# Second-layer attention on one core: the layer norm's last step on another engine, and the next chunk's projections at other steps

## What is computed

```
Q, K, V = relu(x @ Wq + bq), relu(x @ Wk + bk), relu(x @ Wv + bv)      # 16 heads of 8
scores = Q K^T / sqrt(8), masked (causal, and keys whose features sum to 0)
attn = softmax(scores) * query_mask
out = attn V + x
mean, var = mean(out), mean((out - mean) ** 2)                         # over the 128 features
normalized = (out - mean) / sqrt(var + 1e-8)
x = x + gamma * normalized + beta
layer = base_layer + einsum('bdr,bkr->bdk', x_a, x_b)                  # rank 8, one per sequence
x = x + x @ layer                                                      # then a slot-routing FFN
```

## Time and profile before

| | |
|---|---|
| median of 3 runs | 1248.66 us (1247.72 to 1248.96) |
| the profiled execution | 1247.93 us, of it the trace's span 1246.6 us |
| TensorE | 1078.6 us busy (87%) |
| VectorE | 983.2 us busy (79%) |
| ScalarE | 723.0 us busy (58%) |
| GpSimd | 567.7 us busy (46%) |
| the attention stage | first scores at 834.7, its last period begins at 1083.8, next stage at 1146.7 |

### The profile page before, as it was taken

How to read it: one execution, slowest core, us unless ns; L and a number is a source line. 1 busy time by engine, 2 the same in 40 slices (tenths; PEclk the granted TensorE clock), 3 DMA queues, 4 the chain that set the end, 5 groups by cost and what they waited for, 6 DMA issues and landing times.

```text
span 1246.6 us, 25407 instructions
## 1 busy us (share of the span) xinstructions
PE 1078.6 (87%) x8723; PEld 819.9 (66%) x8723; DVE 983.2 (79%) x3810; ACT 723.0 (58%) x1970; POOL 567.7 (46%) x603
## 2 busy tenths in 40 slices
PE   6999999999999977887599999979788877777997
PEld 5887887878787863322377777767566656553655
DVE  5667787869686865899879999985877787776857
ACT  5776666667666754653574445445666556663343
POOL 2334353534343433456234444447766666664001
PEclk9999999999999998986799999988999898989789
DMA  8000000000000000000000000000000000000002
GB/s 334 2 2 1 2 2 1 2 2 2 1 2 2 2 1 0 1 0 1 0 1 1 1 1 4 8 7 18 19 19 18 11 13 16 19 2 1 1 1 69
DMA packets 8577, 18.32 MB, mean 15 GB/s; under 512 B 1280, under 2 KB 5504, under 8 KB 8064
## 3 DMA queue, kind: packets, MB, share of 16 engines
q1 hardware_dynamic: 8448, 16.69, 3.9%
HBM read 10.39 MB, written 2.10 MB: 10 GB/s over the span
## 4 chain that ended last, share of the span: by engine, by line
PE 43%; DVE 36%; issue 9%; ACT 5%; POOL 5%; DMA 0%; DVEq 0%; ACTq 0%; SPq 0%; POOLq 0%
DVE AR_s L1482 6%; PE PB L406 4%; PE PB L390 4%; PE PB L335 4%; PE PB L373 3%; DVE RR_s L1008 3%; PE PB L240 3%; PE PB L1473 3%; ACT W L354 3%; PE PB L241 3%; PE PB L242 3%; DVE W L345 2%; PE PB L1501 2%; DVE AR_s L1698 2%; PE PB L424 2%
## 5 line engine op out<-in xcount | busy, mean ns | idle before, releaser
L354 ACT ACTIVATE W<-W,small 128x128 f32<-128x128 f32 x512 | 198.7, 391 | 139.9 <-DVE small L345 87.0
L365 POOL TENSOR_TENSOR W<-W,small 128x512 f32<-128x512 f32 x128 | 133.5, 1043 | 267.9 <-DVE small L359 267.8
L240 PE MATMUL PB<-RR_s 128*128 128x256 f32 (+3 forms) x544 | 177.4, 326 | 4.8 <-DVE AR_s L397 2.7
L241 PE MATMUL PB<-RR_s 128*128 128x256 f32 (+3 forms) x544 | 167.7, 308 | 0.0
L242 PE MATMUL PB<-RR_s 128*128 128x256 f32 (+3 forms) x544 | 167.6, 308 | 0.0
L1489 POOL TENSOR_TENSOR AR_s<-AR_s,small 128x512 f32<-128x512 f32 x128 | 130.4, 1041 | 72.1 <-DVE small L1482 72.1
L996 ACT ACTIVATE AR_s<-PB,W 128x512 f32<-128x512 f32 (+2 forms) x160 | 101.3, 633 | 104.8 <-PE PB L242 78.4
L1482 DVE CUSTOM_DVE_ANT_0 AR_s<-PB,W 128x128 f32<-128x128 f32 x512 | 112.9, 286 | 49.4 <-PE PB L1473 49.1
L1014 DVE TENSOR_TENSOR RR_s<-AR_s,RR_s 128x512 fp32r<-128x512 f32 (+2 forms) x116 | 115.5, 996 | 8.1 <-ACT RR_s L1001 4.3
L345 DVE CUSTOM_DVE_ANT_0 W<-PB,W 128x128 f32<-128x128 f32 x512 | 113.2, 285 | 2.6 <-PE PB L335 0.4
L240 PEld LDWEIGHTS PB<-RR_s 128*128 128x128 f32 x544 | 104.2, 192 | 15.5 <-issue 4.1
(11 more groups left out here) (350 smaller groups left out, 2616.5 us busy)
## 6 DMA issues: line engine op xcount, KB each, us to landing
W<-in_w SPq DMA_DIRECT2D x1, 5841.0 KB, 24.8
XF<-in_xT SPq DMA_DIRECT2D x4, 512.0 KB, 9.1
AR_s<-AR_s SPq DMA_DIRECT2D x32, 64.0 KB, 2.1
out<-XT SPq DMA_DIRECT2D x8, 256.0 KB, 2.7
W<-in_w SPq DMA_DIRECT2D x1, 1088.0 KB, 5.1
W<-in_w SPq DMA_DIRECT2D x1, 1024.0 KB, 7.9
QS<-AR_s SPq DMA_DIRECT2D x12, 64.0 KB, 2.4
KR<-AR_s SPq DMA_DIRECT2D x12, 64.0 KB, 2.1
```

The costliest lines, as they stand in the source:

```text
L240: nc.tensor.matmul(out, lh, rh, start=True, stop=False)
L241: nc.tensor.matmul(out, ll, rh, start=False, stop=False)
L354: e = nc.scalar.activation(SS[r][:, hl], SS[r][:, hl], ACTF.Exp, bias=mx[r][:, h:h + 1], scale=-1.0, accum_out=rc[r][:, h:h + 1])
L365: nc.gpsimd.tensor_tensor(s3, s3, over(rc[r], 2, [128, 4, 128]), ALU.mult).then_inc(s_nrm, 1)
```

## The change

The layer norm's last step goes from VectorE to ScalarE, as scale x in + bias with a column each per token. The bias is minus the mean times the reciprocal root, so GpSimd gets two more small instructions per chunk (the negated means, and the product). The projections of the next chunk move: query from step 5 to 4, sum and key from 7 to 6, the key's product from 8 to 7, the tokens from 10 to 11, the masks from 11 to 12. A step can now hold two of them: at step 4 the query comes ahead of the sum of the finished chunk.

```diff
+        lmean = xsum
...
+        PROJECT = {4: "query", 6: "key", 7: "keysum", 11: "tokens", 12: "masks"}
+        FINISH = {0: "root", 1: "apply", 3: "gamma", 5: "x3T", 6: "select", 8: "add"}
+
         def aside(s):
 
             c, i = divmod(s, 16)
-            if c < 7 and 5 <= i < 12:
-                return "project", c + 1, i - 5
+            if c < 7 and i in PROJECT:
+                yield PROJECT[i], c + 1
...
             c, i = divmod(s - LATE, 16)
-            if 0 <= c < 7 and i < 9:
-                return "finish", c, i
-            return "", 0, 0
+            if 0 <= c < 7 and i in FINISH:
+                yield FINISH[i], c
...
-            if i == 1:
-                dve.wait_ge(s_fl, 3 * c + 3)
-                for b in range(4):
-                    sl = cs(LN[c % 2], b, 128)
-                    t = nc.vector.tensor_scalar(sl, sl, m3[:, q0 + b, 0:1], rstd[:, q0 + b:q0 + b + 1], ALU.subtract, ALU.mult)
-                t.then_inc(s_fd, 1)
...
+        def pool_root5(c):
+            q0, n = 4 * c, 5 * c
+            nc.gpsimd.tensor_tensor(cs(XF, c), cs(XF, c), w("beta").broadcast_to([128, 512]), ALU.add).then_inc(s_fl, 1)
+            pool.wait_ge(s_nb, 2 * (q0 + 3) + 2)
+            nc.gpsimd.tensor_scalar(rstd[:, q0:q0 + 4].unsqueeze(2), m3[:, q0:q0 + 4, 1:2], 1e-8, None, ALU.add).then_inc(s_fl, 1)
+            nc.gpsimd.tensor_scalar(lmean[:, q0:q0 + 4].unsqueeze(2), m3[:, q0:q0 + 4, 0:1], -1.0, None, ALU.mult).then_inc(s_fl, 1)
+            pool.wait_ge(s_fl, n + 2)
+            nc.gpsimd.tensor_tensor(rstd[:, q0:q0 + 4], rstd[:, q0:q0 + 4], mhalf, ALU.pow).then_inc(s_fl, 1)
+            pool.wait_ge(s_fl, n + 4)
+            nc.gpsimd.tensor_tensor(lmean[:, q0:q0 + 4], lmean[:, q0:q0 + 4], rstd[:, q0:q0 + 4], ALU.mult).then_inc(s_fl, 1)
+
+        def act_apply5(c):
+            act.wait_ge(s_fl, 5 * c + 5)
+            for b in range(4):
+                q, sl = 4 * c + b, cs(LN[c % 2], b, 128)
+                t = nc.scalar.activation(sl, sl, ACTF.Identity, bias=lmean[:, q:q + 1], scale=rstd[:, q:q + 1])
+            t.then_inc(s_ln, 1)
+
+        def pe_gamma5(c):
+            pe_drained5(("T", c))
+            pe.wait_ge(s_ln, c + 1)
```

More of the change, by code:

```diff
@@ L1444, in plan5 @@
                     passes5(("oT", q - 2), 6, s_nd, 4 * (q - 2) + 4)
-            for i in range(9):
-                plan_aside("finish", 7, i)
+            for what in FINISH.values():
+                plan_aside(what, 7)
         plan5()
@@ L1656, in dve_factors @@
                 nc.vector.tensor_tensor(XBP[i - 1], out[:, 0:128], w("lb2b"), ALU.add).then_inc(s_facd, 1)
[L1660 to L1685, removed]
@@ L1739, in step_of @@
         def step_of(table, s):
-            what, c, i = aside(s)
-            if what in table:
-                table[what](c, i)
-        HIDDEN = {3: 5, 4: 6, 8: 7}
+            for what, c in aside(s):
+                if what in table:
+                    table[what](c)
+        HIDDEN = {"gamma": 5, "x3T": 6, "add": 7}
         def pe_attend2():
@@ L1753, in pe_attend2 @@
             pe_S5(0)
[L1754 removed]
+            pe_tokens5(0)
             pe_v5(0)
@@ L1758, in pe_attend2 @@
             nc.tensor.matmul(bank5("b1")[0:64, 0:1], w("fw1b"), smean, start=True, stop=True).then_inc(s_b1m, 1)
-            beside = {"project": pe_project, "factors": lambda c, i: pe_factors(i), "finish": pe_finish}
+            beside = {"query": pe_query5, "key": pe_key5, "tokens": pe_tokens5, "factors": pe_factors,
+                      "gamma": pe_gamma5, "x3T": pe_x3T, "select": pe_select5, "add": pe_add5}
             for q in range(END5):
@@ L1782, in pe_attend2 @@
                 pe_hidden(c)
-            for i in range(9):
-                pe_finish(7, i)
-                if i in HIDDEN:
-                    pe_hidden(HIDDEN[i])
+            for what in FINISH.values():
+                if what in beside:
+                    beside[what](7)
+                if what in HIDDEN:
+                    pe_hidden(HIDDEN[what])
         def act_attend2():
@@ L1791, in act_attend2 @@
             act.wait_ge(s_kd[0], spreads(0))
-            act_project(0, 5)
-            beside = {"project": act_project, "finish": act_finish}
+            act_tokens5(0)
+            beside = {"query": act_query5, "key": act_key5, "tokens": act_tokens5, "apply": act_apply5, "x3T": act_x3T}
             for q in range(END5):
@@ L1817, in act_attend2 @@
                 act_hidden(c)
-            for i in range(9):
-                act_finish(7, i)
-                if i in HIDDEN:
-                    act_hidden(HIDDEN[i])
+            for what in FINISH.values():
+                if what in beside:
+                    beside[what](7)
+                if what in HIDDEN:
+                    act_hidden(HIDDEN[what])
         def dve_attend2():
@@ L1853, in dve_attend2 @@
                 step_of(beside, 4 * q + 3)
-            for i in range(9):
-                dve_finish(7, i)
+            for what in FINISH.values():
+                if what in beside:
+                    beside[what](7)
         def pool_attend2():
```

184 lines of the change are left out of this document (98 added, 86 removed).

## The result

| | before | after |
|---|---|---|
| median | 1247.81 us (1243.61 to 1248.96, 5 runs) | 1234.56 us (1232.36 to 1237.75, 5 runs) |
| ratio of the runs, 95% interval | | 0.9896 [0.9871, 0.9921] |
| span of the profiled execution | 1246.6 us | 1233.3 us |
| mean granted clock of TensorE | 0.938 | 0.941 |

What follows compares the result with a forecast made beforehand. The prediction took TensorE's waits for the layer norm's last step, on VectorE instructions held by GpSimd, as the bound. Terms summed to -21.1 us: 1226.8 for the profiled execution, 1227.5 us for the median, range 1216 to 1240.

Steps and rivals of the forecast that it cites:

- D, clock aside: Period's long iteration, where TensorE waits for the layer norm: 11.65 to 8.5 us, six times, -18.9 us.
- A, clock aside: Iteration after the long one: its scores take 0.92 us less if the clock holds, six times, -5.5 us.
- clock falls: TensorE dropping to half clock after its shorter stand: two falls in seven at 2.1 us each, +4.2 us.
- C: Iteration before the long one: L1192 leaves VectorE's path, 0.60 us each, q = 6 to 26, -3.6 us.
- B, q = 9 to 25: Iteration with query and finished chunk's sum: bank wait 0.36 and later sum 0.3 us, five times, +3.2 us.
- end, clock aside: Stage's end, q = 31 and the eighth chunk: earlier transposes, fewer blocks at half clock, -4.4 us.
- rival 1: The clock falls in every D: seven falls instead of two, +10.5 us, 1238 us; chance 0.22.
- Rival 2: No hold at the masks and no clock fall: D bound by ScalarE at 7.9 us, 1219.5 us; chance 0.14.
- Rival 5: The change does not do what it says, through table loads or another wait in D: 1247 us; chance 0.04.
- Rival 3: VectorE's gamma step (L1702) is also held by GpSimd's late subtractions: seven times, +2.5 us, 1230 us; chance 0.05.
- Rival 4: ScalarE is the bound if its layer norm instructions take over 1.0 us each: slower, 1254 us; chance 0.05.
- the rule against the change: Skill's rule sending multiplications and additions to VectorE: sum near +8, or 1256 us; chance 0.01, within Rival 4's.

Runs made afterwards that it cites:

- e5: Changed kernel plus 14 transposes of a constant ahead of TensorE's wait at L1692, into the bank it then fills; 1223.05 us, ratio 0.9794.
- e8: e5 plus a GpSimd memset of four columns between the product and the next subtraction, which then starts slightly later; 1223.71 us, ratio 0.9815.
- e9: e5 with ScalarE applying the layer norm twice, the first time into a tile nothing reads; 1238.9 us, ratio 0.994.
- e10: Kernel before, plus 32 transposes into a spare bank ahead of TensorE's wait for the affine tokens; 1233.46 us, ratio 0.99.
- e1: Layer norm's last step on ScalarE as in the change, all projections back at their old steps; 1224.54 us, ratio 0.9808.
- e3: Changed kernel with only the query back at step 5; 1221.94 us, ratio 0.9809.
- e4: Changed kernel with only tokens and masks back at steps 10 and 11; 1226.91 us, ratio 0.9831.

## Why the prediction was right, and where it was not

Term by term, as the prediction put them. The clock's own part is taken from after against e5, and "clock aside" is e5 against before.

| term | forecast | measured |
|---|---|---|
| D, clock aside | -18.9 | -17.8 (70.0 to 52.2) |
| A, clock aside | -5.5 | -3.3 (47.0 to 43.7) |
| clock falls | +4.2 | +8.6 (D 2.9, A 3.8, end 1.9) |
| C | -3.6 | -4.2 |
| first D | +0.9 | +1.0 |
| B, q = 9 to 25 | +3.2 | +4.2 |
| q = 1 and 5 | +3.0 | +3.2 |
| end, clock aside | -4.4 | -5.0 (40.6 to 35.6) |
| sum | -21.1 | -13.1 (the stage; the rounded terms make -13.3) |

**The terms of D and C came true.** The reading behind them was that a TENSOR_SCALAR of VectorE is held to the end of GpSimd's running TENSOR_TENSOR, and that ScalarE isn't held. L1629 at 1.04 and its twin at 0.17, and e8, which turned the one into the other with a delay of a tenth, show it. So do ScalarE's 477 to 493 ns for every ACTIVATE. The Trainium skill (SBUF — State Buffer, SBUF: two separate sides) gives the rule: VectorE and GpSimd share one pair of ports as an exclusive lock, and a VectorE instruction that uses both of its read ports waits for the whole GpSimd instruction, while ScalarE has ports of its own. Beside the subtractions the trace agrees on both; beside the root's power it doesn't (last section), and there the measurement decides. The forecast for the mask instruction (held, D at 8.5 by VectorE's path) came true in the last five D of e5 to a tenth; in the first, q = 7, both instructions were held, 0.9 more than forecast. Two slips of the working partly cancel in it: by its own numbers the hold ends at +5.85 where the masks would have ended at +5.11, 0.74 and not 0.9 (e5's row has 0.87), and L1531's 0.58 went in as 0.5.

**The clock is where it was wrong.** The step was "I take two falls in seven": six of the seven came, after stands of 2.3 to 2.6 us. That was rival 1, *the clock falls in every D*, put at 0.22 and 1238. It came true in its place, and the sign that the prediction gave for being wrong, a granted clock of 0.5 after each D, was seen behind six of them. Its price did not come true. I had 2.1 us for a fall, from scores and three blocks of transposes at half clock. Measured, after against e5, it is 8.6 us in six falls of D and one more in the end. For the five falls at q = 7 to 23 it is 6.75, or 1.35 each; they come at different moments, from 0.34 us before the end of the stand to 1.29 after it, and which part of the 2.1 was hidden by other work wasn't tried. With seven falls at 2.1 the forecast would have been 1238, with seven at the measured price some 1233. My argument against the rival, that the other falls came later in their stands, leaned on six stands that were twice as long (4.5 us), which could tell nothing of a short one; the seventh, of 2.84 us from 1132.76 on, had its fall too. TensorE also stood longer than the forecast 2.1 us, 2.41 in most D, since GpSimd's additions took 0.64 and not 0.5: the subtraction starts at +4.96 instead of +4.8. With a row that showed a fall after 2.1 us and none that showed a short stand without one, the likely case was the fall.

**A was a reading of one period.** The 8.21 of the earlier trace rows is the long kind. A over the six periods before is 7.83 on the mean, three of them 7.3 to 7.6, so less was there to win: -3.3, not -5.5.

**B was short by 0.2 each.** I had 0.36 for the bank (the rows that I named give 0.30; 0.36 came true) and 0.3 for the sum of the features. The row 1052.59 shows the first wait, and the row 1056.21 starts 0.51 us behind the one ahead of it, where before the change it was 0.23. Each costs 0.1 more, since a matmul behind a wait takes 0.96 to the next one (1052.59 to 1053.55) where it takes 0.86 in a running sequence (1059.06 to 1059.92 before).

**Rival 2** (no hold at the masks) did not come by itself. e8 made it by hand, and D was 8.2 without the hold, not 7.9. **Rival 5** (1247) did not come either.

**Rival 3 fell**, and on a mistake in reading. L1698 (L1702 before) took 0.74 under a running subtraction, against 0.75 with GpSimd idle. GpSimd beside the L1698 shown above:

```profile
1005.64 2.03 POOL L1497 TENSOR_TENSOR AR_s<-AR_s,small 128x512 f32<-128x512 f32 x2
```

I had counted two inputs in SBUF; gamma is one column, an operand per partition, and the product is read from PSUM, so it has one input tensor in SBUF. The Trainium skill (VectorE: DVE Perf Modes, What auto-detection actually checks) gives the mode with both read ports only to an instruction with a single source that has source and destination in SBUF; the mask instructions fit it, L1698 doesn't, and the trace sorts these two so.

**Rival 4 and the rule against the change.** An ACTIVATE took 0.48, the price forecast, far below the point of decision, 1.0 us. That point itself wasn't tested: e9, with 3.2 us per chunk, is faster than the kernel before but not than e10. The rule that sends additions and multiplications to VectorE (the Trainium skill, ScalarE: Activation LUTs, Rules for kernel authors) would have given +8. The move alone, e1, gave -23.7 by the medians and -18.3 in the stage, so the measurement decides against it here. The rule prices an instruction by itself. VectorE's cost 0.75 here instead of 0.33, each ending with a GpSimd instruction beside it.

**Not settled.** The medians of e3 and e4 lie 12.6 and 7.7 us below the changed kernel's, their stages 7.5 and 3.8. In e4 2.1 us of the rest lie ahead of the stage, in e3 5.3 behind it; why is open. Two of e3's six executions took 1227.8 and 1227.9 us with a mean clock of 0.941, the other four 1218.3 to 1222.3 with 0.944 to 0.947, so the falls of one kernel seem to differ from one execution to the next. Also why q = 27 kept its clock, with the same stand of 2.41 us as q = 19, wasn't tried.

## What to carry to other kernels

Where VectorE's small instructions show two durations, look at what GpSimd runs at that moment, and price a move to ScalarE by the held duration. Price TensorE's half clock behind every stand as its own term, and test it with a few transposes into a bank that is about to be overwritten, before anything is redesigned: here that alone was worth as much as the change. Take a change of several steps apart: one step (the key) paid, two (the query, the masks) cost more than it, and together the moved projections took back 5 of the 18 us that the layer norm's move had won in the stage.

## What the runs showed of the hardware that was not expected

- **The clock fell at stands of 2.2 to 2.6 us**, in six of seven D in the changed kernel, and in seven, six and five of seven in e1, e3 and e4. Those that kept it are q = 27 after, q = 31 in e3, and q = 7 and 23 in e4, so neither the place nor the length of the stand decides it alone. The fall can come after TensorE is at work again: 0.84 us after in the D shown above. The row of e9's timeline at 1040.83 comes with a fall just ahead of it, though fourteen transposes stood ahead of the same stand:

```profile
1040.50:1041.00 0.50, 0.17 (x1) 0.17 (x2) 0.33 (x2) 0.50 (x2) 0.50 (x2) 0.75 0.00 0
1041.00:1042.00 1.00, 1.00 (x6) 1.00 (x7) 0.00 (x0) 1.00 (x3) 1.00 (x2) 0.50 0.00 0
```

- **0.02 us decide over 0.87.** Whether a VectorE instruction of four elements starts just ahead of GpSimd's subtraction or just behind it is the difference of L1630 in e8 (0.17 us) and L1629 in e5 (1.04).
- **Not every neighbour holds, and not every VectorE instruction is held.** In the kernel before, L1544 took 0.84 us in all 22 places where it began under a subtraction. It took 0.23 in all seven where it began under the root's power L1720, a TENSOR_TENSOR too, as here beside the L1720 of the earlier trace rows:

```profile
1039.69 0.23 DVE L1544 TENSOR_SCALAR small<-small 128x16 f32<-128x16 f32 x1
```

  The reciprocal of the same size just ahead of it (L1542) took 0.25 in all 22 places under a subtraction, as it did with GpSimd idle. So the prediction's rule holds for pairs of instructions, not for all of VectorE's beside all of GpSimd's; it was right to leave the power out, and why the power doesn't hold L1544 is open.
- **A GpSimd product of four elements takes 0.20 us, its power of four elements 1.08** (L1679, L1677). I had bounded the product by the power; the operation sets the price, not the size.
